# A decoder stack of three attentions: where the last layer's probabilities are transposed, where the feed-forward inputs are turned, and where the weights' remainders are made

## The reference

```python
# module 0 (self-attention, cross-attention, feed-forward)
q = (q_in @ wq + bq); k = (k_in @ wk + bk); v = (v_in @ wv + bv)     # 16 heads of 64
attn = softmax(where(mask, q @ k.T, -inf) / sqrt(64))
x = layer_norm((attn @ v) @ wo + bo + residual)                      # for sa, then for ca
x = layer_norm(relu(x @ ffn_w1 + ffn_b1) @ ffn_w2 + ffn_b2 + x)
# module 1 (cross-attention with rotary positions)
q = rope(x @ Wq) / sqrt(64); k = rope(ctx @ Wk); v = ctx @ Wv
attn = softmax(where(mask, q @ k.T, -1e9))
y = layer_norm(x + (attn @ v) @ Wo)
```

## Time and profile before

| | |
|---|---|
| median of 3 runs | 585.73 us (585.62 to 585.77) |
| the profiled execution | 584.04 us, its span 582.3 us |
| PE busy | 526.4 us, 90% |
| DVE busy | 446.9 us, 77% |
| ACT busy | 342.0 us, 59% |
| POOL busy | 302.2 us, 52% |
| granted TensorE clock, mean | 0.985 |

### The profile page before, as it was taken

One profiled execution on the slowest core, in us unless ns is written; L12 is line 12 of the kernel. 1 busy time (PEld: TensorE's weight loads), 2 busy tenths in 40 slices (PEclk: granted clock), 3 DMA queues, 4 the chain that ended last, 5 costly groups with the idle time before them and its releaser, 6 DMA issues.

```text
span 582.3 us, 23604 instructions
## 1 busy us (share of the span) xinstructions
PE 526.4 (90%) x10336; PEld 476.6 (82%) x10336; DVE 446.9 (77%) x796; ACT 342.0 (59%) x873; POOL 302.2 (52%) x572
## 2 busy tenths in 40 slices
PE   7789999999998999999999997897878998999995
PEld 6578889999988889889898886887777887888885
DVE  4977977777777677777787888596849899898973
ACT  6366566757775675575645864454544565556553
POOL 2622634454453454263352648385646677667744
PEclk9989999999998999999999999899989999999999
DMA  8900000000111100000000000000000000000000
GB/s 254 303 3 3 3 1 3 2 3 2 40 38 37 30 13 2 2 3 2 3 2 3 2 2 3 2 3 2 7 2 8 12 8 7 8 12 8 7 13 15
DMA packets 10837, 12.73 MB, mean 22 GB/s; under 512 B 752, under 2 KB 8432, under 8 KB 10736
## 3 DMA queue, kind: packets, MB, share of 16 engines
q1 hardware_dynamic: 10736, 11.24, 6.4%
HBM read 10.18 MB, written 1.05 MB: 19 GB/s over the span
## 4 chain that ended last, share of the span: by engine, by line
PE 67%; DVE 17%; POOL 5%; ACT 5%; issue 5%; DMA 1%; SPq 0%; POOLq 0%; ACTq 0%; DVEq 0%
PE ps_p L581 13%; PE ps_p L429 9%; PE ps_p L431 7%; PE ps_p L430 7%; PE ps_p L553 6%; DVE probs L896 5%; PE ps_a L501 4%; PE ps_a L483 4%; POOL qT L1002 3%; DVE turn L787 3%; PE ps_a L465 3%; PE ps_p L546 2%; PE ps_p L606 2%; PE ps_p L548 2%; PE ps_p L547 2%
## 5 line engine op out<-in xcount | busy, mean ns | idle before, releaser
L1020 POOL TENSOR_TENSOR small<-mv,epsilon 128x1 f32<-128x1 f32 x48 | 18.1, 378 | 191.0 <-DVE mv L826 191.0
L581 PE MATMUL ps_p<-wo,headsT 128*128 128x128 f32 x768 | 96.0, 279 | 1.8 <-ACT headsT L650 1.3
L581 PEld LDWEIGHTS ps_p<-wo,headsT 128*128 128x128 f32 x768 | 93.1, 196 | 3.6 <-ACT headsT L650 1.4
L787 DVE TENSOR_TENSOR turn<-ps_p,rope 128x1024 f32<-128x1024 f32 x64 | 76.2, 1218 | 6.9 <-PE ps_p L431 3.9
L691 ACT ACTIVATE probs<-ps_a,top 128x64 f32<-128x64 f32 x256 | 56.4, 360 | 41.4 <-DVE top L855 41.4
L881 DVE TENSOR_REDUCE total<-probs 128x16 f32<-128x1024 f32 x48 | 58.2, 1212 | 23.4 <-ACT probs L701 20.7
L660 ACT ACTIVATE probsT<-ps_p 128x512 f32<-128x512 f32 x96 | 54.3, 612 | 35.3 <-PE ps_p L553 35.3
L678 ACT ACTIVATE headsT<-ps_a 128x512 f32<-128x512 f32 x60 | 32.6, 595 | 68.0 <-PE ps_a L501 68.0
L429 PE MATMUL ps_p<-xT_hi,wq_hi 128*128 128x256 f32 x192 | 60.9, 317 | 10.6 <-DVE turn L787 4.8
L553 PE MATMUL ps_p<-eye,probs 128*128 128x128 f32 x384 | 55.1, 275 | 12.8 <-DVE probs L896 6.3
L553 PEld LDWEIGHTS ps_p<-eye,probs 128*128 128x128 f32 x384 | 43.7, 141 | 23.2 <-issue 11.8
(11 more groups left out here) (139 smaller groups left out, 1400.2 us busy)
## 6 DMA issues: line engine op xcount, KB each, us to landing
out<-y_out SPq DMA_DIRECT2D x16, 64.0 KB, 1.5
X<-in_x SPq DMA_DIRECT2D x1, 768.0 KB, 8.4
across<-in_across SPq DMA_DIRECT2D x1, 704.0 KB, 10.6
wq_raw<-in_L_xattn_sa_wq SPq DMA_DIRECT2D x2, 256.0 KB, 3.1
wk_raw<-in_L_xattn_sa_wk SPq DMA_DIRECT2D x1, 512.0 KB, 4.9
wv_raw<-in_L_xattn_sa_wv SPq DMA_DIRECT2D x1, 512.0 KB, 7.2
wo<-in_L_xattn_sa_wo SPq DMA_DIRECT2D x1, 512.0 KB, 8.3
wo<-in_L_xattn_ca_wo SPq DMA_DIRECT2D x1, 512.0 KB, 9.5
```

What stands on the lines that cost most here:

```text
L581: last = mm(bank[:, 0:E], headsT[:, p, :, :].rearrange("r b q -> r (b q)"), wo[:, layer % 2, p, :], start=(p == 0), stop=(p == PAIRS - 1))
L787: ins = V.tensor_tensor(turn[:, j % 2, :, :].rearrange("d a (h b t) -> d a h b t", h=2, t=S), bank[:, None, :].broadcast_to([128, 2, 512]) ...
```

## The change

Three things are moved; no instruction of arithmetic is added or taken out.

1. `defers(u)`: for steps 32 to 45 the transposes of unit u-1's probabilities are left out of step u and made in step u+1 as "PP", right behind the scores and ahead of all other fills. The heads of the same step then wait for them. Two waits are added: ACT's exponentials (steps 33 to 45) and DVE's shift and ACT's exponentials (step 46) overwrite the half of `probs` that PP still reads, so they wait for PP to be filled.
2. In the steps with rotary projections the feed-forward's input (FT, steps 31, 33, 35) is transposed ahead of the projections, not behind them; ACT and DVE empty it in the same place of their orders.
3. `weights` goes behind the sum and one eviction in the ordinary steps (13, 14, 16, 29), to the end of step 30, and between the second and the third rotary product in step 32. In the odd steps with rotary projections DVE's part of T goes behind the sum.

```diff
@@ -81,12 +81,18 @@
     return attends(u) and rotary(u)
 
 
+def defers(u):
+
+    return by_head(u) and u > 2 * UNITS - 1
+
+
 def fills(u):
 
     heads = [("O", b, "A") for b in range(2)] if heads_in_ring(u) else []
     turn_in = [("T", 0, "AD")] if u % 2 == 0 and projected(u) is not None and not by_head(u) else []
     values = [("V", j, "A") for j in range(2)] if attends(u) else []
-    probabilities = [("P", j, "A") for j in range(2)] if turns(u) else []
+    probabilities = [("P", j, "A") for j in range(2)] if turns(u) and not defers(u) else []
+    deferred = [("PP", j, "A") for j in range(2)] if defers(u - 1) else []
     result = [("Y", 0, "D")] if finishes(u) else []
     project = []
     if projected(u) is not None:
@@ -100,7 +106,7 @@
 
         ffn = [("FT", 0, "AD")], [("F1", 0, "A"), ("F1", 1, "A")], [("F2", 0, "D")]
         into, inside, outof = ffn if ffn_chunk(u) is not None else ([], [], [])
-        return project[:2] + heads + project[2:] + into + values + inside + result + probabilities + outof + next_in
+        return deferred + into + project[:2] + heads + project[2:] + values + inside + result + probabilities + outof + next_in
     if ffn_chunk(u) is not None:
         k = len(project) // 2
         return heads + early[:1] + [("FT", 0, "AD")] + early[1:] + probabilities + project[:2] + [("F1", 0, "A")] \
@@ -108,7 +114,7 @@
     if u % 2:
         return heads + early + probabilities + project + result
     k = len(project) // 2
-    return heads + turn_in + early + probabilities + project[:k] + result + project[k:] + late
+    return deferred + heads + turn_in + early + probabilities + project[:k] + result + project[k:] + late
 
 
 class Tally:
@@ -181,11 +187,15 @@
     before = [("norm", u - 1, 0), ("norm", u - 1, 1)] if by_head(u - 1) else []
     ffn_out = [("fout", 0)] if ffn_chunk(u - 1) is not None else []
     if by_head(u):
-        return [("max", 0)] + ([] if split_heads(u) else [("max", 1)]) + [("weights", 0)] + emptied[:4] + before + emptied[4:] \
-            + ffn_out + [("sum", 0)]
-    head = [("max", 0)] + ([] if split_heads(u) else [("max", 1)]) + before + [("shift", 0), ("shift", 1), ("weights", 0)]
+        n = 4 if ffn_chunk(u) is None else 5
+        turn_in = [e for e in emptied if fills(u)[e[1]][0] == "T"]
+
+        early, late = ([("weights", 0)], []) if u == 2 * UNITS else ([], [("weights", 0)])
+        return [("max", 0)] + ([] if split_heads(u) else [("max", 1)]) + emptied[:n - 2] + early + emptied[n - 2:n] + before \
+            + [e for e in emptied[n:] if e not in turn_in] + ffn_out + [("sum", 0)] + late + turn_in
+    head = [("max", 0)] + ([] if split_heads(u) else [("max", 1)]) + before + [("shift", 0), ("shift", 1)]
     n = 1 if u % 2 == 0 and projected(u) is not None or ffn_chunk(u) is not None else 0
-    return head + emptied[:n] + [("sum", 0)] + emptied[n:n + 1] + [("norm", u, 0)] + emptied[n + 1:n + 2] \
+    return head + emptied[:n] + [("sum", 0)] + emptied[n:n + 1] + [("weights", 0), ("norm", u, 0)] + emptied[n + 1:n + 2] \
         + [("norm", u, 1)] + emptied[n + 2:] + ffn_out
 
 
@@ -488,7 +498,10 @@
             def weight_values(u):
                 w, last = u - 2, None
 
-                pe.wait_ge(act_emptied, EMPTY_A.at(u - 1, "P", 1))
+                if defers(u - 1):
+                    pe.wait_ge(act_emptied, EMPTY_A.at(u, "PP", 1))
+                else:
+                    pe.wait_ge(act_emptied, EMPTY_A.at(u - 1, "P", 1))
                 if heads_in_ring(u):
                     for b in range(2):
                         bank_free(u, head_at(u) + b)
@@ -546,12 +559,13 @@
                     mm(bank[:, :], x[0], w[0], start=True, stop=False)
                     mm(bank[:, :], x[0], w[1], start=False, stop=False)
                     last = mm(bank[:, :], x[1], w[0], start=False, stop=True)
-                elif name == "P":
-                    pe.wait_ge(normed, NORMED.at(u - 1, j))
+                elif name in ("P", "PP"):
+                    unit = u - len(name)
+                    pe.wait_ge(normed, NORMED.at(unit, j))
                     for pp in range(HALF):
                         at_head = 2 * (HALF * j + pp)
                         last = nc.tensor.transpose(bank[:, 128 * pp:128 * pp + 128],
-                                                   probs[:, (u - 1) % 2, at_head:at_head + 2, :].rearrange("q h k -> q (h k)"),
+                                                   probs[:, unit % 2, at_head:at_head + 2, :].rearrange("q h k -> q (h k)"),
                                                    eye[:, :])
                 elif name[0] in "QK":
                     n_w = "QK".index(name[0])
@@ -679,6 +693,9 @@
                       .then_inc(headed, 1)
 
             def exponentials(u, j):
+                if j == 0 and defers(u - 1):
+
+                    act.wait_ge(filled, FILL.at(u, "PP", 1))
                 if by_head(u):
                     act.wait_ge(dve_step, VSTEP.at(u, "max", 0) if split_heads(u) else VSTEP.at(u, "eighth"))
                     for n in range(8 * j, 8 * j + 8):
@@ -738,7 +755,7 @@
                 for at, (name, j, who) in enumerate(fills(u)):
                     if "A" not in who:
                         continue
-                    if waiting and name not in ("O", "T"):
+                    if waiting and name not in ("O", "T", "PP"):
                         exponentials(u, waiting.pop(0))
                     empty(u, at, name, j)
                     if name == "T":
@@ -863,6 +880,9 @@
                         V.tensor_scalar(top[:, :], top[:, :], -float(D) ** -0.5, None, ALU.mult).then_inc(dve_step, 1)
 
             def shift(u, j):
+                if j == 0 and defers(u - 1):
+
+                    dve.wait_ge(filled, FILL.at(u, "PP", 1))
                 dve.wait_ge(dve_step, VSTEP.at(u, "max", 0 if split_heads(u) else j))
                 if split_heads(u):
                     V.tensor_tensor(probs[:, u % 2, :, :].rearrange("q (f m) k -> q m f k", m=4)[:, 2 * j:2 * j + 2, :, :],
```

## The result

The changed kernel takes **562.42 us** in the median of four runs (562.09 to 563.51); the kernel before takes 585.67 beside it on the same chip (583.93 to 585.77). The profiled executions are 563.51 against 584.04, a gain of 20.5 us. The first maximum, ahead of everything that was changed, begins at 17.02 us and not 15.61, so 22.0 us were won from there on. The 1.4 is no effect of the change: the changed kernel run again begins it at 16.08.

What follows compares the result with a forecast made beforehand. Neither DVE (10.52 us of 11.70) nor PE (10.58) was the bound alone; they waited for each other. Terms summed to 19.5 us off the profiled 584.04, giving 564.5, plus 1.7 for the median: 566.2 us, range 560 to 575.

Steps and rivals of the forecast that it cites:

- the second: Rival: steady steps don't move, PE held by xT_lo behind the sum and POOL by its turn buffer; 572.5 us, chance 0.10.
- the third: Rival: turning first does nothing, the heads wait for x2T_lo's bank instead; 572 to 575 us, chance 0.06.
- the fourth: Rival: slower, as exponentials wait for the transposes and the next scores for the exponentials; 590 us, chance 0.03.
- steps 36 to 45: Steady steps: DVE's idle time mostly goes, even steps 10.83 us and odd 11.07; gain 5.6 us, bounds 0 and 7.
- step 16: Remainder wv_lo moved: 1.0 us from PE's wait for cT_lo, plus 0.8 for half the half-clock cost.
- steps 30 and 31, with wk_lo: wk_lo leaves step 30 for before step 31's maximum, input turned first: gain 1.25 us, bounds -0.3 and 3.1.
- step 32: wv_lo between second and third rotary product, held up by POOL's additions: -0.35 us, bounds +0.3 and -1.1.
- step 33: Feed-forward step with x2T_lo turned first, PE no longer waiting for it: 17.98 to 14.65 us, gain 3.3.
- step 34: DVE's 1.58 us wait for late scores at its end, hidden by PE's lead: gain 1.45 us, bounds 0 and 1.6.
- step 35: Feed-forward step turned first, both half-clock stretches gone: gain 6.3 us, bounds 3.3 and 6.8.
- Rival 1: The clock keeps falling: step 16 and both stretches of step 35 stay slow; 570 to 571 us, chance 0.15.
- over 1 us in even steps: Sign that the forecast is wrong: PE waiting for xT_lo for over 1 us in even steps.

Runs made afterwards that it cites:

- the remainders alone: The kernel before with only the six `weights` remainders moved, no deferral and no turning first: 583.08 us, ratio 0.996.
- the best version: The changed kernel with xT_lo ahead of the sum again and wq_lo back ahead of the sum in step 29, timed again: 559.51 us, ratio 0.958.
- the one with wq_lo back: The changed kernel with xT_lo ahead of the sum and wq_lo ahead of the sum in step 29, first timing: 560.52 us, ratio 0.958.

## Why the prediction was right, and where it was not

The mechanism was right in all three parts. Of the rivals, the second is out because the steady steps moved, the third because turning first gave 4.0, 2.4 and 6.0 us alone, and the fourth because steps 36 to 45 got 5.9 shorter in sum. Term by term, in us of gain on the profiled execution:

| term | forecast | measured |
|---|---|---|
| step 14 | 1.0 | 0.84 |
| step 16 | 1.8 | 2.48 |
| step 29 | -0.85 | -0.95 |
| steps 30 and 31, with wk_lo | 1.25 (to 3.1) | 3.72 |
| step 32 | -0.35 | -0.66 |
| step 33 | 3.3 | 2.78 |
| step 34 | 1.45 | 0.84 |
| step 35 | 6.3 | 6.79 |
| steps 36 to 45 | 5.6 | 5.92 |
| step 46 | 0 | 0.31 |
| start-up, not of the change | 0 | -1.4 |

**The mis-sized term is step 31**, the one outside its bounds. Two things went into it, each too dark by over 1 us. "In step 30 nothing is gained by it", I wrote of wk_lo, because the third rotary product waits for POOL there in any case, and I charged 1.5. But POOL itself was late through wk_lo, by the 0.87 that its addition took longer, so without wk_lo there the wait ended earlier; the cost is 0.27. And of the half clock at 364.7 I wrote "I let that stay". In the changed kernel the clock stays up in this step. The row of z in its timeline of DVE:

```profile
364.14 0.29 DVE L826 TENSOR_TENSOR z<-ps_p,res 128x128 f32<-128x128 f32 x1 [0.98 <-PE ps_p L595]
```

That is 9.7 us after the maximum at 354.47, with an idle time of 0.98 before it; before, the longest of these waits was 5.2, in this step. Turning first alone gives 4.0 us in this step, where I had counted 2.7. With 0.27 and 4.0 the term would have been 3.7, and the forecast 563.7.

**Steps 33 and 35** had 14.65 each and came out at 15.20 and 14.69. The idle time of DVE in step 33, of the changed kernel:

```profile
393.33 0.29 DVE L826 TENSOR_TENSOR z<-ps_p,res 128x128 f32<-128x128 f32 x1 [1.03 <-PE ps_p L595]
...
395.12 0.42 DVE L816 TENSOR_TENSOR fz<-ps_p,fres 128x256 f32<-128x256 f32 x1 [0.95 <-PE ps_p L620]
```

I had said 0.7 and 1.0. That is as close as such a count gets. What is left of the 0.55 is 0.22 for scores that were late, by a pause of PE in the middle of them (below). The half clock of step 35 went with the wait ahead of it, as forecast.

**Steady steps.** The sum of 5.6 was right to 0.3, in part because two misses cancel: the four odd steps gave 5.6 where I had 5.1, and the five even ones lost 0.2, through step 36 (11.44, not 11.10), where I had a gain of 0.1 (five times my own 10.91 to 10.83 would have been 0.4). Step by step I had 10.83 and 11.07, it is 10.90 and 10.84. The deferral alone shows the price, 0.35 per even step, and that the part of the change which caused it bought nothing. I had credited "the 0.97 goes, because the sum now fills the wait" to moving xT_lo. It goes by the deferral: with that alone odd steps are 10.90. The move alone takes it away as well, but gives half of it back in the even steps and the rest in step 36. The number was right and its cause was half wrong.

**Step 32.** My 0.35 was for a wv_lo that is held up by POOL. It was not: it takes 1.24 us (1.40 in the kernels with xT_lo ahead of the sum). POOL's rotary additions beside it were the ones that were held, as the rows show, of the changed kernel (wv_lo and the two additions) and then of before:

```profile
374.99 1.24 DVE L931 TENSOR_TENSOR wv_lo<-wv_raw,wv_hi 128x1024 fp32r<-128x1024 f32 x1
373.87 3.51 POOL L1022 TENSOR_TENSOR qT<-turn 128x512 f32<-128x512 f32 x2 [4.35 <-DVE turn L804]
```

```profile
378.82 2.54 POOL L1002 TENSOR_TENSOR qT<-turn 128x512 f32<-128x512 f32 x2 [4.91 <-DVE turn L787]
```

The Trainium skill ("SBUF — State Buffer", section "Who interferes with whom") has it that the order of issue decides which of the two is blocked. These rows agree: wv_lo had begun at 374.99, and of the two additions the first ended at 375.15 and the second, which takes 1.27 alone, at 377.38, behind the end of wv_lo at 376.23. The loss in the step has another source, the late xT_lo and the half clock behind it: with xT_lo ahead of the sum the step is 12.49, a gain of 0.16, and with the remainders alone it is 12.48.

**Step 16.** I counted half of the 1.6 that the half clock cost. It all came: 0.95 at full clock (12.05 to 11.10), and 1.5 by the clock. PE's wait there is 1.19 now and was 2.13, and in all nine profiles of kernels with the remainders moved the step is 11.1. Rival 1 was right in one respect: waits of over 1 us stay at each special step, and one of 2.25 in step 32 brought one fall of the clock. That wait, for xT_lo, is also the one place where my sign "over 1 us in even steps" came. There is one such stretch between 350 us and the last microsecond where I had named three as the sign against me, and two when the changed kernel was run again. Against this rival I had said that the falls shown follow waits of over 2 us. The fourth of before, at 419.3 in step 35, came behind a pause of 1.53 (last section).

**Step 34** gave 0.84 and not 1.45. The 1.58 at its end came of a pause of PE in the scores of step 35, and it went because that pause now stands in the scores of step 34 (last section). There PE's lead hid all but 0.22 of it from the maximum, as forecast, but the first projection came 0.56 late behind it.

The start-up is 1.4 longer, in code that was not changed. It differs between executions of one program as well: the first maximum begins at 17.02 and 16.08 in the two profiles of the changed kernel, and at 16.24 and 17.86 in those of the best version. It belongs to no term of the sum. Without the start-up the profiled gain is 22.0, and that of the medians is 23.3, which is 3.8 more than the sum of 19.5.

## What to carry to other kernels

When two engines wait for each other in turn, find the instruction whose result is needed a whole step later than the order asks for it, and defer that: here the deferral of eight transposes gave 7.4 us in ten steps, and most of the rest came from serving first what an idle engine was waiting for. Of a wait that you are about to fill with other work, ask whether the engine was early or the path was late; moved alone, xT_lo gained half of the wait that it filled and lost that again behind a feed-forward step, and on top of the deferral it cost 2.3 us. And where banks go round in a ring, a tile's place in the order also decides which engine must empty its bank: the transposes two places further back cost 39 us, the clock's share in it included.

## What the runs showed of the hardware

A wait of PE of the same length does not always bring the clock down. In step 16 the wait of 2.13 for cT_lo was followed by 3.4 us at 0.50 in three kernels (before, the deferral alone, xT_lo alone), and the same wait of 2.12 by none with the input turned first. The step is 13.6 to 13.7 in the first three and 12.05 in the last, so a term of 1.5 us hung on something that the wait's length does not show.

PE stops in a stream of small matmuls with nothing to wait for that the profile shows. These are the last ten score matmuls of step 34, of the changed kernel, and then of the best version, where the transposes behind them ran at half clock:

```profile
395.36 1.46 PE L475 MATMUL ps_a<-kT,qT 32*64 32x64 f32 x118
398.70 0.35 PE L475 MATMUL ps_a<-kT,qT 32*64 32x64 f32 x10 [1.88 <-issue]
398.98 1.09 PE L567 MATMUL ps_p<-eye,probs 128*128 128x128 f32 x8
```

```profile
395.89 0.50 PE L475 MATMUL ps_a<-kT,qT 32*64 32x64 f32 x10 [1.60 <-issue]
396.32 1.97 PE L567 MATMUL ps_p<-eye,probs 128*128 128x128 f32 x8
```

The pause is before the same ten matmuls in six of the seven profiles of the changed kernel and of the versions made from it that keep its order of PE (1.24 to 1.88 us; the one with normalising behind the maximum has none). It is not new. The kernel before has it too, in the scores of step 35, and so do the three made from it without the deferral; the 1.58 of the earlier trace rows is DVE waiting for it:

```profile
415.22 1.38 PE L465 MATMUL ps_a<-kT,qT 32*64 32x64 f32 x108
418.13 0.45 PE L465 MATMUL ps_a<-kT,qT 32*64 32x64 f32 x20 [1.53 <-issue]
```

These four have a second one, in the heads of step 46 (1.2 to 1.7 us); the changed kernel does not, and that step is 0.31 shorter. The kernel with the deferral alone has neither. What the pause costs is decided by the clock behind it. In the changed order it fell in three of the six (xT_lo ahead of the sum, the best version, the changed kernel run again), and there step 34 took 13.3 to 13.4 us; it did not in the others, which took 11.5 to 11.9. The best version and the one with wq_lo back are the same program, 13.29 and 11.54 in this step: those 1.8 us are not in the code. That is why no version here is told from another by the total alone where the steps differ by less. What causes the pause stays open, but its place points somewhere: counted in all of PE's recorded instructions, the pause in the scores stands at number 14274 in those four kernels and at 13762 in the six, 512 apart. One queue of the profile (q8) brought instructions in 82 loads of 16 KB, which is one for every 257 of PE's 21057. A load had begun 0.5 to 1.2 us ahead of each of these pauses (at 396.32 for the one from 396.82 on). Nearly all other loads passed without a pause, so this is where to look and not a cause that was shown.
